# Decoder with six sub-layers on one core: buffers for the late value products, and the written orders of three queues

## The reference, cut to what matters

```python
# L0 FFN; act_qdq rounds by a scale from the peak of the whole tensor
x = act_qdq(x)
up = act_qdq(x @ lpbq_dequant(w_up).T)
gate = act_qdq(x @ lpbq_dequant(w_gate).T)
sig = fixed_qdq_u16(jax.nn.sigmoid(gate))
gate = act_qdq(gate * sig)                 # "t" in the kernel
o = act_qdq(gate * up)                     # "v" in the kernel
return o @ lpbq_dequant(w_down).T
# L1 cross-attention: k and v come from the context alone
kv = ctx @ Wkv
k, v = jnp.split(kv, 2, axis=-1)           # 16 heads of 64
k = l2norm(k) * k_scale
out = (softmax(q @ k.T * 8) @ v) @ Wout    # per head, then layernorm
```

## Time and profile before

| | |
|---|---|
| time, median of 3 runs | 1490.17 us (1486.34 to 1495.93) |
| time of the profiled execution | 1493.76 us |
| its span | 1492.0 us |
| VectorE busy | 1040.3 us, 70% |
| TensorE busy | 1291.4 us, 87% |
| ScalarE busy | 520.7 us, 35% |
| GpSimd busy | 271.3 us, 18% |
| transfers | 104.66 MB, mean 70 GB/s |

### The profile page before, as it was taken

How to read it: one execution, slowest core, us unless ns; L and a number is a source line. 1 busy time by engine, 2 the same in 40 slices (tenths; PEclk the granted TensorE clock), 3 DMA queues, 4 the chain that set the end, 5 groups by cost and what they waited for, 6 DMA issues and landing times.

```text
span 1492.0 us, 17934 instructions
## 1 busy us (share of the span) xinstructions
PE 1291.4 (87%) x7132; PEld 879.5 (59%) x7132; DVE 1040.3 (70%) x1974; ACT 520.7 (35%) x602; POOL 271.3 (18%) x188
## 2 busy tenths in 40 slices
PE   7899999998599999755276899999999999998964
PEld 4566777766544554322155567676768676766653
DVE  3678888885234489846734478787969788787674
ACT  2233333432234477654501232233232323232310
POOL 0111111110000000014200031322304141313241
PEclk9999999996689999876679999999999999999997
DMA  4000000000161054487512101111100200000000
GB/s 187 15 14 29 29 29 26 18 15 0 56 241 71 31 195 154 133 305 274 190 57 92 62 31 52 55 50 52 55 29 29 72 28 12 33 19 32 0 15 14
DMA packets 47059, 104.66 MB, mean 70 GB/s; under 512 B 10496, under 2 KB 31104, under 8 KB 43648
## 3 DMA queue, kind: packets, MB, share of 16 engines
q1 hardware_dynamic: 42816, 101.42, 19.6%
q10 hardware_dynamic: 4160, 2.10, 0.5%
HBM read 59.47 MB, written 44.04 MB: 69 GB/s over the span
## 4 chain that ended last, share of the span: by engine, by line
PE 73%; DVE 14%; ACT 5%; issue 5%; DMA 2%; POOL 1%; SPq 0%; POOLq 0%; DVEq 0%; ACTq 0%
PE ps L1120 7%; PE ps L1180 6%; PE ps L1009 6%; PE ps L846 6%; PE ps L785 5%; PE ps L896 4%; PE ps L692 4%; PE ps L1153 3%; PE ps L1067 2%; PE ps L801 2%; PE ps L765 2%; PE ps L1091 2%; PE ps L1102 2%; DMA vw_scratch<-arena 2%; PE ps L1197 2%
## 5 line engine op out<-in xcount | busy, mean ns | idle before, releaser
L1180 PE MATMUL ps<-arena 128*128 128x256 f32 x512 | 119.9, 389 | 6.7 <-ACT arena L1573 6.7
L1600 POOL TENSOR_TENSOR arena<-arena 128x4 f32<-128x4 f32 x48 | 49.2, 1025 | 378.3 <-DVE arena L1759 378.3
L1120 PE MATMUL ps<-arena 128*128 128x512 f32 x256 | 117.6, 598 | 0.0
L1180 PEld LDWEIGHTS ps<-arena 128*128 128x128 f32 x512 | 98.7, 195 | 27.8 <-ACT arena L1573 10.2
L1009 PE MATMUL ps<-arena 128*128 128x256 f32 x384 | 89.6, 394 | 26.8 <-DVE arena L2020 24.6
L2065 DVE TENSOR_TENSOR arena<-ps,arena 128x2048 f32<-128x2048 f32 x32 | 73.3, 2292 | 39.4 <-PE ps L1067 39.1
L1663 POOL TENSOR_TENSOR arena<-arena 128x16 f32<-128x16 f32 x32 | 91.9, 2907 | 34.1 <-DVE arena L2094 34.1
L1009 PEld LDWEIGHTS ps<-arena 128*128 128x128 f32 x384 | 75.1, 199 | 38.1 <-issue 25.0
L846 PE MATMUL ps<-arena 128*128 128x512 f32 x192 | 85.6, 604 | 0.0
L896 PE MATMUL ps<-arena 128*128 128x512 f32 x192 | 84.7, 595 | 0.0
L785 PEld LDWEIGHTS ps<-arena 128*128 128x128 f32 x512 | 66.4, 210 | 18.5 <-ACT arena L1268 15.3
(11 more groups left out here) (246 smaller groups left out, 2652.0 us busy)
## 6 DMA issues: line engine op xcount, KB each, us to landing
v_scratch<-arena SPq DMA_DIRECT2D x7, 1536.0 KB, 5.7
arena<-v_scratch SPq DMA_DIRECT2D x7, 1536.0 KB, 6.9
up_scratch<-arena SPq DMA_DIRECT2D x6, 1536.0 KB, 7.3
arena<-up_scratch SPq DMA_DIRECT2D x6, 1536.0 KB, 7.5
arena<-x_scratch SPq DMA_DIRECT2D x16, 512.0 KB, 4.3
vw_scratch<-arena SPq DMA_DIRECT2D x32, 256.0 KB, 4.4
arena<-vw_scratch SPq DMA_DIRECT2D x8, 1024.0 KB
arena<-x SPq DMA_DIRECT2D x8, 512.0 KB, 4.1
```

Source lines behind the costliest of these rows:

```text
L1120: last = mm(flat(p % 2), w["cos_wq"][:, k, p * P:(p + 1) * P], xt4[:, k], start=k == 0, stop=k == NC - 1)
L1180: last = mm(flat(2)[:, C:2 * C], cos_pt[:, p], cos_vw[:, par, p], start=p == 0, stop=p == NP - 1)
L1600: g.tensor_tensor(var[0], var[1], neghalf[:, 0:NT], ALU.pow)\
```

## The change

`VW_LATER` is 11: value products 0 to 10 are copied into `vw_out` as before, 11 to 15 in turn into two new buffers (1024 words each, behind `kst` in the slot of the v stored second) and `vw_out`: buffers 1, 2, 0, 1, 2. Each buffer has its own semaphore for the landing of its stores, and a copy waits for the last store from its own buffer. The first copy into the new place waits until that v is stored. At the second loop's start one wait on the stores becomes three. The lists of calls of ScalarE, TensorE and SyncE for the late part are written anew.

```diff
--- before.py
+++ after.py
@@ -318,6 +318,7 @@
         ksq = ar.take(INNER)
         ar.at = keep + V_ORDER[1] * NF * T
         kst = ar.take(NP, P)
+        vw_bufs = (vw_out, ar.take(2, 2, C), ar.take(2, 2, C))
 
         ar.at = keep
         dn_v = ar.take(NT, NF, P)
@@ -408,6 +409,16 @@
             if not b.before(back):
                 eng.wait_ge(moved(name, par), b.half(16, moved_before(name) + 16 - 8 * back))
 
+        VW_LATER = 11
+
+        def vw_at(n):
+
+            return 0 if n < VW_LATER else (n - VW_LATER + 1) % 3
+
+        def vw_before(n):
+
+            return sum(vw_at(m) == vw_at(n) for m in range(n))
+
         def wait_all_moved(eng, name, even=B // 2, odd=B // 2):
             for par, n in enumerate((even, odd)):
                 eng.wait_ge(moved(name, par), moved_before(name) + 16 * n)
@@ -525,8 +536,8 @@
                 sp.wait_ge(ev("vw_copied"), n + 1)
                 for half in range(2):
                     sp.dma_start(vw_units[n // 2, n % 2, half],
-                                 vw_out[half * TC:half * TC + TC].rearrange("p r i c -> p (r i) c"))\
-                        .then_inc(ev("vw_stored"), 16)
+                                 vw_bufs[vw_at(n)][half * TC:half * TC + TC].rearrange("p r i c -> p (r i) c"))\
+                        .then_inc(ev(f"vw_stored_{vw_at(n)}"), 16)
 
             sp.wait_ge(sig("gate_done", NF).sem, sig("gate_done", NF).at(Batch(B - 1), NF))
             sp.wait_ge(ev("ctx_stored"), 16)
@@ -569,29 +580,29 @@
                 sp.dma_start(v_rows[V_ORDER[q]], gated[:, V_ORDER[q]].rearrange("p (t n) -> p t n", t=NT))\
                     .then_inc(moved("v_stored", q % 2), 16)
 
+            store_vw(6)
             load_up(2)
-            store_vw(6)
             load_up(3)
             store_vw(7)
             store_v(0)
             load_up(4)
             store_vw(8)
             store_v(1)
+            load_up(5)
             store_vw(9)
-            load_up(5)
             store_v(2)
+            load_up(6)
             store_vw(10)
-            load_up(6)
-            store_vw(11)
             store_v(3)
             load_up(7)
+            store_vw(11)
             store_vw(12)
             store_v(4)
             store_vw(13)
             store_v(5)
             store_vw(14)
+            store_vw(15)
             store_v(6)
-            store_vw(15)
             wait_all_moved(sp, "v_stored", 4, 3)
 
 
@@ -612,7 +623,8 @@
                 if b.first():
                     sp.wait_ge(ev("pads_cleared"), 1)
                     sp.wait_ge(ev("ck_stored"), 16 * 4)
-                    sp.wait_ge(ev("vw_stored"), 32 * 2 * NP)
+                    for k in range(3):
+                        sp.wait_ge(ev(f"vw_stored_{k}"), 32 * sum(vw_at(m) == k for m in range(2 * NP)))
                 wait_back(sp, "cos_scored", b, 2, NT)
                 for lo, hi in ((0, CD), (CD, P)):
                     sp.dma_start(cos_kb[lo:hi, par, :, lo:hi], ck_d[lo:hi, :, at])\
@@ -970,24 +982,24 @@
             value_products(7)
             values(4)
             value_products(8)
+            key_rows(0)
             value_products(9)
-            key_rows(0)
             values(5)
             key_rows(1)
             value_products(10)
-            value_products(11)
             turn_keys(0)
             key_rows(2)
+            value_products(11)
             values(6)
             value_products(12)
             turn_keys(1)
             key_rows(3)
             value_products(13)
             values(7)
+            value_products(14)
             turn_keys(2)
-            value_products(14)
+            value_products(15)
             turn_keys(3)
-            value_products(15)
 
 
             pe.wait_ge(ev("cos_k_scaled"), 4)
@@ -1362,9 +1374,12 @@
             def copy_vw(n):
 
                 act.wait_ge(ev("vw_done"), n + 1)
-                if n:
-                    act.wait_ge(ev("vw_stored"), 32 * n)
-                f(vw_out.rearrange("p r i c -> p (r i) c"), rows2(6), ACT.Copy).then_inc(ev("vw_copied"), 1)
+                if vw_before(n):
+                    act.wait_ge(ev(f"vw_stored_{vw_at(n)}"), 32 * vw_before(n))
+                if n == VW_LATER:
+                    act.wait_ge(moved("v_stored", 1), moved_before("v_stored") + 16)
+                    wait(act, "v_ready", Batch(2))
+                f(vw_bufs[vw_at(n)].rearrange("p r i c -> p (r i) c"), rows2(6), ACT.Copy).then_inc(ev("vw_copied"), 1)
 
             early, late = tuple(range(NF // 2)), tuple(range(NF // 2, NF))
             copy_metric()
@@ -1453,43 +1468,43 @@
                 act.dma_start(ck_d[:, :, g * P:(g + 1) * P], kst).then_inc(ev("ck_stored"), 16)
 
             copy_values(3)
+            copy_vw(6)
             ffn_round_up(0)
-            copy_vw(6)
             ffn_round_up(1)
+            ffn_round_t(0)
             copy_vw(7)
-            ffn_round_t(0)
             copy_values(4)
             ffn_round_t(1)
             ffn_round_up(2)
             copy_vw(8)
-            copy_vw(9)
             ffn_round_up(3)
             copy_keys(0)
+            ffn_round_t(2)
+            copy_vw(9)
             copy_values(5)
-            ffn_round_t(2)
+            ffn_round_up(4)
             copy_keys(1)
+            ffn_round_t(3)
             copy_vw(10)
-            ffn_round_up(4)
-            copy_vw(11)
-            ffn_round_t(3)
             store_keys(0)
             copy_keys(2)
+            ffn_round_up(5)
+            copy_vw(11)
             copy_values(6)
-            ffn_round_up(5)
+            ffn_round_t(4)
             copy_vw(12)
-            ffn_round_t(4)
             store_keys(1)
             copy_keys(3)
+            ffn_round_up(6)
             copy_vw(13)
-            ffn_round_up(6)
             copy_values(7)
             ffn_round_t(5)
+            copy_vw(14)
             store_keys(2)
-            copy_vw(14)
             ffn_round_up(7)
+            copy_vw(15)
             ffn_round_t(6)
             store_keys(3)
-            copy_vw(15)
             ffn_round_t(7)
```

## The result

The changed kernel takes 1475.03 us in the median of four runs (1474.31 to 1478.39), the kernel before 1491.47 in four (1486.34 to 1495.93): a ratio of 0.9899, 95% interval 0.9881 to 0.9917. The prediction was 1474, with 1466 to 1487 as its range.

A forecast was written before the change was run, and what follows sets the result against it. ScalarE, stalled before copies awaiting store landings and key projections, was taken to set the late part's pace; reordered starts bring its end from 740.64 to 724.5, 16 us off: 1477.8 from the profiled 1493.76, 1474 against the median; range 1466 to 1487.

The forecast's parts named there:

- The start: ScalarE at the late part's start: copy 6 ahead of up's roundings, product 0 at 639.1 instead of 644.86, 5.8 us earlier.
- waits for landings under 4 us in all: Sign of being right: ScalarE's copies of value products wait under 4 us in all for stores to land.
- The waits for the projection: ScalarE's copies of keys 2 and 3 would still wait for TensorE's key projection, some 6 us at keys 2.
- The term for the projection itself: TensorE's key projections 2 and 3 counted at 6.46 us, with TensorE at its lower level.
- case D: TensorE runs projection 3 partly at its upper level, say 4.3 us: gain 18, 1472; chance 0.52 together with the forecast.
- Rival A: GpSimd's roots and sums collide with VectorE's products, keys late next: gain 10 us, 1480; chance 0.22.
- I expect the order to be the larger half: Late part: buffers touch only 6.8 us of waits at copies 11 to 15; order moves the 5.35 and 8.26 away.
- Rival B: Landings stretch, copies 8, 9 and 10 on one buffer each wait 3 us: gain 7, 1483; chance 0.15.
- 28.1 MB in 92 us: Late part's transfers: the same bytes in 92 us rather than 108, share 0.73 up to about 0.86.
- Rival C: Transfers become the bound; over 1% slower from 228 GB/s on, end at 755, 1505; chance 0.06.
- The stretch after it shifted without change: Sign of being right: the stretch after the late part, with the second loop, only shifts in time.

The follow-up runs named there:

- start_only: Kernel before with copy 6 ahead of the roundings of up, copy 7 behind the first rounding of t, store 6 ahead of load 2; 1486.36 us, ratio 0.9964.
- changed_again: The changed kernel run once more beside the other kernels on one chip, with no edit; 1475.25 us, ratio 0.9894.
- orders_only: Kernel before with the three new lists of calls, but one buffer and one semaphore; 1486.07 us, ratio 0.9970.
- stores_twice: Changed kernel with every store of value products sent a second time, 5.2 MB more in the late part; 1491.76 us in one run.
- start_and_keys0: start_only plus the changed kernel's moves around keys 0 on ScalarE, TensorE and SyncE, still one buffer; 1482.13 us, ratio 0.9933.
- t_first_keys_late: Changed kernel with later roundings of t earlier, copies of keys 2, 3 behind roundings of up 5, 6, their sums behind products 4, 6; 1470.59 us, ratio 0.9857.

## Why the prediction was right

**The size.** 16 us were forecast for the late part, 18.1 and 17.4 measured in two profiles; the medians moved by 16.4. That these come so close to 16 is partly luck, as the late part gave more and the profiles gave 2 us back behind it (below). Two of the recorded figures don't follow from their own terms: with half of 9.6 us the range would be 1467 to 1488, and a gain of 15 to 21 us is 1469 to 1475, not 1478. The steps, in us after the scale:

| step | forecast | measured |
|---|---|---|
| product 0 | 10.2 | 10.9 |
| copy of keys 0 | 23.4 | 24.1 |
| copy of keys 2 | 46.3 | 45.8 |
| copy of keys 3 | 62.9 | 59.5 |
| product 5 | 71.0 | 67.6 |
| product 7 | 88.0 | 85.9 |
| end | 95.6 | 93.6 |

The sum closes: product 5 came 3.4 us earlier than forecast and took 1.3 us longer, which leaves the 2.0 us at the end.

**The start** was right: from the start of copy 5 to that of copy 6, with the landing of store 5 between, it was 5.2 us, as forecast. Copy 6 began 1.6 us after the scale, 0.8 us later than forecast, because copy 5 began 3.57 us ahead of the scale and not 4.36. The sign "waits for landings under 4 us in all" was missed by little: 4.6 us, of which 2.0 lie ahead of the scale. start_only shows this step by itself.

**Keys 2 and 3.** The waits for the projection stayed, 5.44 and 3.79 us. The term for the projection itself was mis-sized: I took 6.46 us for both, from a row with a mean granted clock of 0.57. That of keys 2 took 5.35 us at 0.69, and that of keys 3 took 3.70 us at 1.00. The second is case D, and accounts for 2.8 of the 3.4 us at copy of keys 3. In changed_again they took 6.38 and 3.70 us; its copy of keys 2 comes 0.7 us later than here, and so does its end.

**Collisions.** Rival A's mechanism is there, its price is not. Two roots of key norms took 5.95 and 6.00 us, off the path. Product 5 took 4.65 us, on the path, 1.3 us more than the forecast counted. The prediction watched the roots only; what product 5 met was the scaling behind the root, and in the kernel before, where product 5 took 4.49 us, it was the scaling as well (715.07 to 716.97). So against the kernel before the collision cost next to nothing. In changed_again product 4 took 4.70 us too, off the path. GpSimd's scaling of keys 3 ran from 692.88 to 694.78, and the product started inside it:

```profile
654.45 6.00 POOL L1662 TENSOR_TENSOR arena<-arena 128x16 f32<-128x16 f32 x1 [1.62 <-DVE arena L2004]
...
692.88 1.90 POOL L1665 TENSOR_TENSOR arena<-arena 128x1024 f32<-128x1024 f32 x1
```

694.78 + 3.36 is 698.14, and it ended at 697.99; the root that began at 654.45 ended at 660.45, 2.8 us after product 2 had ended at 657.63. Each time the later one was held until the earlier was through, and then took its usual 3.36 or 2.90 us to within 0.15 us. The Trainium skill, SBUF — State Buffer, section Who interferes with whom, calls the contention of the two engines for their shared ports an exclusive lock, counts VectorE instructions with two inputs in SBUF among those that contend with GpSimd's reads, and says that the order of issue decides who blocks; the trace agrees, and shows for two inputs that the later one waits for the whole of the earlier.

**Order or buffers.** Here the reasoning failed. "I expect the order to be the larger half" counted for the buffers only the waits that the old order had, 6.8 us. orders_only shows that the new order makes copies 12 and 15 wait 5 us each if there is one buffer: the order alone is worth 6.6 us in the late part and the buffers 5.7, about the same. The sum was right since it was made for both together.

**Transfers.** Rival B did not come: copies 8 and 9 waited 0.2 and 0.8 us. The term "28.1 MB in 92 us" was right (share 0.85, forecast 0.86). stores_twice puts the margin at less than 5.2 MB. Rival C did not come either: the last v landed 5.9 us ahead of the scale of v.

**After the part.** "The stretch after it shifted without change" did not quite hold. From v's scale to the end it is 751.4 us in the one profile of before, 751.2 in start_only and 751.0 in orders_only; it is 753.4 and 753.6 in two of the changed kernel and 753.3 to 754.5 in the six others with new buffers (stores_twice set aside). That would look like a price of the buffers' waits, but start_and_keys0, whose second loop is that of the kernel before to the letter, has 753.4 as well. What goes with it in every case is the clock. In the first 110 us of this stretch the mean granted clock was 0.86 in the three short ones and 0.83 to 0.85 in all others, and TensorE was busy for 670.4 to 670.7 us of 750 in the short ones and 672.8 to 676.1 in the others, at the same 4448 products. Single groups go both ways: 48 products of the down projection take 13.41 us before and 12.38 after, the eight of the metric projection 5.47 and 6.64. What sets on which side a run falls stays open. So the 2 us go with the clock and not with the code of the second loop; whether the new late part sets them off is not shown.

## What to carry to other kernels

When engines work through written lists, look at what stands directly behind each waiting instruction, and move what is needed soonest ahead of it: here the same roundings, merely ahead of a copy of keys, gave 6.6 us more. Price a buffer with the waits that the new order would have without it, not with those that the old order had. A chain of starts worked out from rows, instruction by instruction, was good to 3.4 us in 94 here; the waits taken alone, 6.8 us for the buffers, did not show what the two halves give together.

## What the hardware showed that I had not expected

- GpSimd took 5.98 us from its last elementwise operation to the exchange over partitions (t_first_keys_late), though the same routine had run four times in the launch: a pair of MODIFY_POOL_CONFIG stands ahead of the exchange each time that elementwise operations came before it. A kernel that ends such a chain just ahead of a reduction on GpSimd pays for it.
- A one-element operation on VectorE with two inputs took 0.60 to 1.90 us instead of 0.16 when it met an operation of GpSimd, and a product 5.02 us instead of 3.36 when it met GpSimd's square of keys in t_first_keys_late (673.98 to 675.87). VectorE of that kernel:

```profile
672.70 1.33 DVE L1995 TENSOR_TENSOR arena<-arena 128x1 f32<-128x1 f32 x1
674.07 5.02 DVE L1991 TENSOR_TENSOR arena<-arena 128x3072 f32<-128x3072 int16 x1
...
682.51 0.16 DVE L1995 TENSOR_TENSOR arena<-arena 128x1 f32<-128x1 f32 x1
```
